# Products with C in three buffers of their own, and one reduction over all eight states

## The reference, cut to what matters

```python
proj = hidden_states @ W_in.T                  # (2, 64, 4096)
u, gate = jnp.split(proj, 2, axis=-1)
u = jax.nn.silu(conv(u) + conv_b)              # depthwise, 4 taps
dt, Bm, Cm = jnp.split(u @ Wx.T, [R, R + N], axis=-1)    # each rms-normed
delta = jax.nn.softplus(dt @ Wdt.T + dt_bias)
def step(state, xs):
    d_t, B_t, C_t, u_t = xs
    dA = jnp.exp(d_t[..., None] * A)
    state = dA * state + (d_t * u_t)[..., None] * B_t[:, None, :]
    y_t = jnp.einsum('bdn,bn->bd', state, C_t)
    return (state, y_t)
y = ys + u * D_param
y = y * jax.nn.silu(gate)
return y @ W_out.T
```

## Time and profile before

| | us |
|---|---|
| median of three runs | 373.48 |
| the profiled execution | 374.15 |
| its span (first to last instruction) | 372.4 |
| TensorE busy | 336.3 (90%) |
| VectorE busy | 267.0 (72%) |
| ScalarE busy | 206.0 (55%) |
| GpSimd busy | 107.7 (29%) |
| DMA, 81.85 MB, mean rate | 220 GB/s |

### The profile page before, as it was taken

The page is one execution under the profiler, slowest core; times in us unless marked ns, Lnnn a source line. Parts: engine busy times, 40 slices in busy tenths (PEclk is TensorE's granted clock), DMA queues, the critical chain, the costliest instruction groups (busy, mean ns, idle before and its releaser), DMA issues.

```text
span 372.4 us, 5061 instructions
## 1 busy us (share of the span) xinstructions
PE 336.3 (90%) x1928; PEld 215.4 (58%) x1928; DVE 267.0 (72%) x362; ACT 206.0 (55%) x402; POOL 107.7 (29%) x75
## 2 busy tenths in 40 slices
PE   0688999999899999999499999899999999899996
PEld 0334664653555555555165776687343577787795
DVE  2877887647979989886556698995721798975381
ACT  1985633189999999880702774463022468350350
POOL 2501000026988988888000020202000020300000
PEclk9999999999999999999699999999999999999999
DMA  6999999753030020661147799589999995000001
GB/s 243 423 422 419 420 325 422 283 212 113 2 110 6 0 113 3 225 243 46 57 127 271 285 396 400 215 329 352 393 429 363 427 422 236 2 2 2 0 2 56
DMA packets 12966, 81.85 MB, mean 220 GB/s; under 512 B 2109, under 2 KB 2365, under 8 KB 3661
## 3 DMA queue, kind: packets, MB, share of 16 engines
q1 hardware_dynamic: 11614, 78.23, 53.9%
q10 hardware_dynamic: 1296, 3.22, 2.3%
q0 software_dynamic: 32, 0.07, 0.1%
HBM read 80.86 MB, written 0.52 MB: 219 GB/s over the span
## 4 chain that ended last, share of the span: by engine, by line
PE 66%; DVE 17%; ACT 7%; DMA 6%; issue 2%; POOL 1%; SPq 0%; DVEq 0%; ACTq 0%
PE psum L1063 11%; PE psum L1002 8%; PE psum L1295 7%; PE psum L1138 7%; PE psum L1180 6%; DMA ring<-in_ctx 6%; PE psum L1215 4%; PE psum L1009 4%; PE psum L959 3%; DVE rounded L1727 3%; ACT arena L793 3%; PE psum L1414 2%; PE psum L1449 2%; PE psum L1190 2%; DVE arena L1671 2%
## 5 line engine op out<-in xcount | busy, mean ns | idle before, releaser
L793 ACT ACTIVATE arena<-arena 128x126 f32<-128x126 f32 x256 | 76.6, 394 | 3.2 <-DVE arena L1671 2.9
L1671 DVE TENSOR_TENSOR_SCAN arena<-arena,psum 128x1024 f32<-128x1024 f32 x24 | 54.6, 2281 | 5.8 <-PE psum L1138 5.0
L630 POOL TENSOR_TENSOR arena<-arena 128x1024 f32<-128x1024 f32 x23 | 54.3, 2365 | 8.4 <-DVE arena L1671 8.4
L571 POOL TENSOR_TENSOR small<-small 128x1 f32<-128x1 f32 x6 | 9.6, 1608 | 144.2 <-DVE small L1498 138.6
L1063 PE MATMUL psum<-ring,hT 128*128 128x512 f32 x104 | 50.2, 605 | 0.8 <-ACT hT L694 0.8
L1727 DVE TENSOR_TENSOR rounded<-ring,rounded 128x2048 fp32r<-128x2048 f32 x16 | 36.5, 2286 | 15.9 <-ACT rounded L820 15.9
L820 ACT ACTIVATE rounded<-ring 128x2048 fp32r<-128x2048 f32 x16 | 30.5, 1913 | 17.8 <-PE psum L1009 10.5
L1138 PE MATMUL psum<-plain 64*128 64x512 f32 x128 | 36.1, 641 | 0.4 <-DVE plain L1671 0.3
L1063 PEld LDWEIGHTS psum<-ring,hT 128*128 128x128 f32 x104 | 17.8, 190 | 21.9 <-issue 20.8
L1180 PEld LDWEIGHTS psum<-ident,arena 128*128 128x128 f32 x192 | 22.0, 141 | 11.7 <-issue 9.7
L1002 PE MATMUL psum<-rounded,split 128*128 128x512 f32 x96 | 24.7, 399 | 2.4 <-DVE rounded L1727 1.8
(11 more groups left out here) (237 smaller groups left out, 595.3 us busy)
## 6 DMA issues: line engine op xcount, KB each, us to landing
ring<-in_w_in SPq DMA_DIRECT2D x16, 1024.0 KB, 15.2
ring<-in_ctx SPq DMA_DIRECT2D x13, 1024.0 KB, 10.8
ring<-in_w_out SPq DMA_DIRECT2D x8, 1024.0 KB, 4.8
ring<-in_ctx_t SPq DMA_DIRECT2D x7, 1024.0 KB, 5.9
ring<-in_w_base SPq DMA_DIRECT2D x4, 1024.0 KB, 4.9
ring<-in_x_wk SPq DMA_DIRECT2D x4, 1024.0 KB, 9.8
ring<-in_a_wo SPq DMA_DIRECT2D x4, 1024.0 KB, 11.5
ring<-in_x_wq SPq DMA_DIRECT2D x3, 1024.0 KB, 9.0
```

The costliest lines, as they stand in the source:

```text
L630: pool.tensor_tensor(state[s % STATES], state[s % STATES], c, ALU.mult).then_inc(product_ready, 1)
L793: last = act.activation(to, of, ACT.Exp, scale=a_par[:, k, state_no:state_no + 1])
L1671: dve.tensor_tensor_scan(state[s % STATES], dA[:, s % 3, :], psum[:, p:p + 2, :].rearrange("p a b -> p (a b)"), 0.0, ALU.mult, ALU.add).th ...
```

## The change

- `state` has three buffers, at other addresses, and three new buffers `product` take the place of the in-place result. GpSimd (and VectorE for step 31) reads `state` in order (batch, state, time) and writes `product` in order (state, batch, time), so one block of 128 columns is one state of both batches. It waits for the sum of step `s - 3` before it writes; the scan waits for the product of step `s - 3` in place of the sum of step `s - 4`.
- `state_sum` adds all eight blocks in one place: eight transposing matmuls as before, into 128 columns per tile. `copy_y` copies 256 columns in place of 512. `fold_y` is two plain transposes in place of four float32 products.
- ScalarE: the last `gate_tanh` stands ahead of `decay(31)`; `gated_high(2)` moves from ahead of `decay(31)` to behind `high(0)`; the load of `bk` moves from step 26 to behind the last decay, after a wait for all of GpSimd's products, which replaces the wait for the sum of step 28.
- VectorE: `gated_low(2)` moves from ahead of `copy_y(7)` to behind `low(0)`; `gate_y` gets one more wait (`yg_ready`).

```diff
--- before.py
+++ after.py
@@ -43,7 +43,7 @@
 HN = NS // 2
 STEPS = 2 * DT
 DIRECT = 1
-STATES = 4
+STATES = 3
 QUAD = 4
 
 U_SPLIT = (2, 3, 4)
@@ -192,7 +192,8 @@
         sg = carve(arena, 6240, DT, P)
         cwide = carve(arena, 8288, NS * P)
         dA = carve(arena, 10336, 3, HN * P)
-        state = [plain[:, 3 * HN * P:4 * HN * P]] + [carve(arena, 13408 + HN * P * i, HN * P) for i in range(STATES - 1)]
+        state = [carve(arena, 19040, HN * P), carve(arena, 23296, HN * P), plain[:, 3 * HN * P:4 * HN * P]]
+        product = [carve(arena, 13408 + HN * P * i, HN * P) for i in range(STATES)]
         cdiag = carve(arena, 23296, NS, L)
         ident2 = carve(arena, 24320, L)
         proj = carve(arena, 16480, 3, UN)
@@ -627,7 +628,11 @@
                     pool.wait_ge(c_rest, 3)
                     pool.wait_ge(c_ready, 1)
                 c = cwide[:, HN * P * (s % 2):HN * P * (s % 2) + HN * P]
-                pool.tensor_tensor(state[s % STATES], state[s % STATES], c, ALU.mult).then_inc(product_ready, 1)
+                if s >= STATES:
+                    pool.wait_ge(reduced, s - STATES + 1)
+                pool.tensor_tensor(product[s % STATES].rearrange("p (n b t) -> p b n t", n=HN, b=B),
+                                   state[s % STATES].rearrange("p (b n t) -> p b n t", b=B, n=HN),
+                                   c.rearrange("p (b n t) -> p b n t", b=B, n=HN), ALU.mult).then_inc(product_ready, 1)
                 if s % QUAD == 2 and s >= 10:
                     gate_y(s // QUAD - 2)
                 if s == 1:
@@ -820,6 +825,8 @@
                 act.activation(unit_halves[m % 3][:, 0, :, :], slot(split_units[m]), ACT.Copy).then_inc(unit_high, 1)
 
             for s in range(3, STEPS):
+                if s - 1 == GATE_AT[-1]:
+                    gate_tanh(NG - 1)
                 decay(s)
                 if s - 1 in Z_AT:
                     softplus_exp(2 + Z_AT.index(s - 1))
@@ -828,12 +835,10 @@
                     du_copy(DU_AT.index(s - 1) + 1)
                 if s == 17:
                     proj_copy(6)
-                if s - 1 in GATE_AT:
+                if s - 1 in GATE_AT[:-1]:
                     gate_tanh(GATE_AT.index(s - 1))
                 if s == 29:
                     proj_copy(7)
-                if s == 30:
-                    gated_high(GATE_HALF)
                 if s == 26:
 
                     act.wait_ge(du_copied, NG)
@@ -841,15 +846,16 @@
                     act.dma_start(w_ar, dram["w_ar"]).then_inc(rank_in, 16)
                     act.dma_start(b_base, dram["b_base"].to_broadcast([P, D])).then_inc(bias_in, 16)
                     act.dma_start(bq, dram["bq"].to_broadcast([P, D])).then_inc(bias_in, 16)
-                    act.dma_start(bk, dram["bk"].to_broadcast([P, D])).then_inc(bias_in, 16)
 
 
             high(0)
+            gated_high(GATE_HALF)
             act.wait_ge(gated, NB)
             act.dma_start(permi, dram["perm_row"].to_broadcast([P, D])).then_inc(perm_in, 16)
             act.dma_start(perm_coli, dram["perm_col"]).then_inc(perm_in, 16)
             act.wait_ge(dbu_ready, STEPS)
-            act.wait_ge(reduced, STEPS - STATES + 1)
+            act.wait_ge(product_ready, STEPS - 1)
+            act.dma_start(bk, dram["bk"].to_broadcast([P, D])).then_inc(bias_in, 16)
             high(1)
             gated_high(3)
             for m in range(2, 7):
@@ -1173,21 +1179,19 @@
                     pe.wait_ge(delta_ready, q + 1)
                 if q >= 2:
                     pe.wait_ge(y_skipped, q - 1)
-                for b in range(B):
-                    to = 2 * P * (s // 2 % 2) + P * b
-                    for n in range(HN // 2):
-                        of = P * HN // 2 * b + P * n
-                        last = pe.matmul(psum[:, y_bank(q), to:to + P], state[s % STATES][:, of:of + P], ident[:, :],
-                                         start=(s % 2 == 0 and b == 0 and n == 0), stop=(s % 2 == 1 and n == HN // 2 - 1),
-                                         is_transpose=True, skip_group_check=True)
+                to = P * (s // 2 % 2)
+                for n in range(HN):
+                    last = pe.matmul(psum[:, y_bank(q), to:to + P], product[s % STATES][:, P * n:P * n + P], ident[:, :],
+                                     start=(s % 2 == 0 and n == 0), stop=(s % 2 == 1 and n == HN - 1), is_transpose=True,
+                                     skip_group_check=True)
                 last.then_inc(reduced, 1)
 
             def fold_y(q):
 
                 pe.wait_ge(y_copied, q + 1)
-                for n in range(2 * B):
+                for n in range(2):
                     of = UN * (q % 2) + P * n
-                    last = pe.matmul(psum[:, y_bank(q), L * n:L * n + L], h[:, of:of + P], ident2, start=True, stop=True)
+                    last = pe.transpose(psum[:, y_bank(q), P * n:P * n + P], h[:, of:of + P], ident[:, :])
                 last.then_inc(y_folded, 1)
 
             for s in range(2, STEPS):
@@ -1666,7 +1670,7 @@
                 dve.wait_ge(dA_ready, s + 1)
                 dve.wait_ge(dbu_ready, s + 1)
                 if s >= STATES:
-                    dve.wait_ge(reduced, s - STATES + 1)
+                    dve.wait_ge(product_ready, s - STATES + 1)
                 p = input_bank(s, 0)
                 dve.tensor_tensor_scan(state[s % STATES], dA[:, s % 3, :], psum[:, p:p + 2, :].rearrange("p a b -> p (a b)"),
                                        0.0, ALU.mult, ALU.add).then_inc(scan_done, 1)
@@ -1674,14 +1678,17 @@
             def times_c(s):
                 dve.wait_ge(scan_done, s + 1)
                 c = cwide[:, HN * P * (s % 2):HN * P * (s % 2) + HN * P]
-                dve.tensor_tensor(state[s % STATES], state[s % STATES], c, ALU.mult).then_inc(dve_prod, 1)
+                dve.wait_ge(reduced, s - STATES + 1)
+                dve.tensor_tensor(product[s % STATES].rearrange("p (n b t) -> p b n t", n=HN, b=B),
+                                  state[s % STATES].rearrange("p (b n t) -> p b n t", b=B, n=HN),
+                                  c.rearrange("p (b n t) -> p b n t", b=B, n=HN), ALU.mult).then_inc(dve_prod, 1)
 
             def copy_y(q):
 
                 dve.wait_ge(reduced, QUAD * (q + 1))
                 if q >= 2:
                     dve.wait_ge(y_folded, q - 1)
-                dve.tensor_copy(h[:, UN * (q % 2):UN * (q % 2) + UN], psum[:, y_bank(q), :]).then_inc(y_copied, 1)
+                dve.tensor_copy(h[:, UN * (q % 2):UN * (q % 2) + 2 * P], psum[:, y_bank(q), 0:2 * P]).then_inc(y_copied, 1)
 
             def skip_y(q):
 
@@ -1695,6 +1702,7 @@
             def gate_y(q):
 
                 dve.wait_ge(y_skipped, q + 1)
+                dve.wait_ge(yg_ready, q)
                 v = slice(2 * q, 2 * q + 2)
                 dve.tensor_tensor(sg[:, v, :], sg[:, v, :], uc[:, v, :], ALU.mult).then_inc(yg_ready, 1)
 
@@ -1739,9 +1747,9 @@
 
             skip_y(STEPS // QUAD - 2)
             gate_y(STEPS // QUAD - 2)
-            gated_low(GATE_HALF)
             copy_y(STEPS // QUAD - 1)
             low(0)
+            gated_low(GATE_HALF)
             skip_y(STEPS // QUAD - 1)
             gate_y(STEPS // QUAD - 1)
             low(1)
```

## The result

The changed kernel takes 361.77 us (median of four runs, 361.74 to 361.82); the kernel before took 373.70 in the four runs beside it. The ratio is 0.9678, 95% interval 0.9661 to 0.9695. The forecast was 361.4, with 360.2 to 365.0 as range.

A forecast was written before the change was run, and what follows sets the result against it. TensorE was taken to bound the late quads, with a hole and half clock at the stage's end; -6.03 - 2.66 + 0.75 - 2.95 - 1.18 = -12.07 gave 362.1 profiled, 361.4 us as median, range 360.2 to 365.0.

The forecast's parts named there:

- a fold saves 0.59: TensorE's folds: two transposes for four float32 products save 0.59 us each; folds 1 to 5 give -2.95 us.
- The hole, -6.03: Stage end: with the last tanh ahead of decay(31), the first output product needs no wait for silu, -6.03 us.
- The half clock, -2.66: First six output records: with no hole, no half clock behind it, 5.24 less 2.58, -2.66 us.
- The new wait, +0.75: TensorE then waits at fold_y(6), behind three outputs, for scan 31, times_c and copy_y(6), +0.75 us.
- Folds 6 and 7, -1.18: These two folds stand in TensorE's full list and save 2 x 0.59, -1.18 us.
- The sum, -12.07: All terms together: -12.07 us, taking the profiled execution from 374.15 to 362.1 us.
- The median, 361.4: Forecast median of the changed kernel, the profiled 362.1 less the 0.67 by which runs lay below the profiled one.
- A: Rival: ScalarE and VectorE set the stage, so the folds' 2.95 us gain is hidden; 364.4 us, chance 0.10.
- B: Rival: a half-clock stretch still meets the outputs, so 2.66 us comes back; 364.1 us, chance 0.11.
- C: Rival: GpSimd's products become the bound, deciding from 3.04 us each on; slower, chance 0.04.
- D: Rival: turn(7) still late or decays pushed behind, so scan 31 gains less; 363.4 us at 2 us, chance 0.07.
- Cost nothing: Claim that the moved `bk` load, product 30 wait, gated_high(2), gated_low(2) and gate_y's new wait add no time.

The follow-up runs named there:

- a: The kernel before with only the new order of the last tanh, gated_high(2), gated_low(2) and gate_y's added wait; 366.57 us, ratio 0.9803.
- b: The changed kernel with the kernel before's order of tanh, rounding and decays put back; products, sums and folds as changed; 369.60 us, ratio 0.9883.
- f: The changed kernel with fold_y's two transposes as two float32 products, four records in place of two; 363.53 us, ratio 0.9723.
- c: The kernel before with 22 idle float32 products put into TensorE's hole ahead of the first output product; 373.33 us, ratio 0.9988.
- e: The changed kernel with copy_y(6) ahead of times_c(31) on VectorE instead of behind it; 361.06 us, ratio 0.9656.
- h: The kernel before with 46 transposes of the identity put into TensorE's hole; 373.33 us in the one run.
- g: The changed kernel with gated_high(2) put back between the last tanh and decay(31); 369.36 us, ratio 0.9880.
- d: The changed kernel with gated_high(2) put back ahead of both the last tanh and decay(31); 367.79 us, ratio 0.9835.
- i: Kernel e with two gate products moved from steps 25 and 27 to 3 and 5, a projection copy from step 17 to 13; 359.92 us, ratio 0.9624.

## Why the prediction was right, point by point

- *TensorE bounds the quads; a fold saves 0.59.* Right. Measured 0.84 to 0.22, 0.62. Scan input 29, 168.32 to 165.16, came 3.16 us earlier where 2.95 was forecast. That the first fold counts nothing is right too: scan 9 moved from 112.46 to 112.41. The prediction thought that part of the gain would be hidden up to 140 us; nothing was, fold 3 already came 1.29 earlier (143.77 to 142.48) where two folds are 1.24. Runs a, b and f exclude that the folds are hidden.
- *The hole, -6.03.* Right. TensorE goes from sum 29 straight into the outputs.
- *The half clock, -2.66.* Right inside the sum. The six records take 2.74 in the timeline, the first of them starting before the last sum ends; from the end of the sums (170.82 + 1.97 = 172.79) to their own end (175.37) it is 2.58, as taken. As a separate prize it was mis-sized: c shows 0.83 to 0.93 for it, because VectorE's chain hid the rest. The term and the +0.75 belong together, and a reader who took the -2.66 alone would have been wrong, as the expectation of c was.
- *The new wait, +0.75.* The prediction's own times (copy ends 179.2, TensorE ready at 178.53) give 0.67, so the term was rounded up without a reason given. From where the fold would have started without a wait (172.63 + 2.58 = 175.21) to 175.98 it is 0.77, of which 0.61 show as idle time. e took it away and got 0.71.
- *Folds 6 and 7, -1.18.* 1.24 by the measured fold.
- *The sum, -12.07.* With the measured sizes -3.16 - 6.03 - 2.66 + 0.77 - 1.24 = -12.32; the first split product came 12.31 earlier, the profiled execution 12.41. That the sum fits to the hundredth is chance: counted by ends of records in place of starts, the wait and the two folds come out 0.06 apart. Of the profiled execution the forecast was 362.1, and it took 361.74.
- *The median, 361.4.* Measured 361.77. The step that was off is the carry-over to the median: the profiled execution before lay 0.67 above its runs, and I took that off; that after lies 0.03 below its own. The 0.67 was scatter of one execution: the kernel before ran from 373.43 to 374.41 in the four runs beside the result, the changed one from 361.74 to 361.82. Why the kernel before scatters more was not looked into.
- *Rivals.* A fell (a, b, f). B: the clock is 1.00 in every stretch of the stage in the trace after, and transposes held it up in h. C: GpSimd's product is 2365 and 2362 ns against 2365, far from 3.04 us. D: tanh, decays and scan 31 follow one another within 0.1 us. VectorE's copy of 256 columns is 0.41 (0.40 was taken); its last product into the new order took 1.32 in this trace and 1.22 in that of e, against 1.23 in place before the change and 1.32 in place in a, so the order of the output isn't what moves it.
- *Cost nothing.* gated_high(2), gated_low(2), `bk` and the waits of the three-buffer ring show nowhere as waits of the path. g shows what gated_high(2) costs where the decays stand behind its wait for GpSimd: 7.6 us.

## What to carry to other kernels

At the end of a stage, read for each call in an in-order list what it waits for and who waits for it: a rounding whose result nobody read for some 10 us held up the decays and the tanh on which the whole stage ended. Price the removal of an idle stretch together with the next thing that is late, since a slow clock behind a hole may be hidden and comes out only when the chain beside it moves too. Where an engine is full for many rounds, count its records: six fewer per round were worth what they took, seven times over, and the same for a product moved away, until GpSimd and VectorE were full (i).

## What the runs showed of the hardware

The granted clock fell to the lower of its two levels with TensorE's idle times of 6.03 us (kernel before, b), 6.08 us (g) and 3.71 us (d), not with 0.61 us or 1.13 us (the kernel after, c). In the kernel before it fell while TensorE was still idle: 1.00 from 179 to 180 us, 0.52 from 180 to 181. Transposes slow with it: eight took 1.91 us in g against 1.04. And 46 float32 transposes with nothing else among them kept it up as 22 float32 products did: the first output records behind both took 2.81 us. GpSimd's two-input product took the same 2.36 us whether it wrote in place, into another buffer in rows of 64 words that hop by 512 bytes, or read its input from `arena` or `plain`.
